# An attention and feed-forward layer on one core: the last unit of the output projection stands four steps later, between two products of the feed-forward tail

## The reference, cut to what matters

```python
q, k, v = x @ Wq[h], x @ Wk[h], x @ Wv[h]                  # (b, h, 1024, 64)
attn = softmax(causal(q @ k.T / sqrt(64)))
heads = attn @ v                                           # 16 heads side by side: (b, 1024, 1024)
y  = x + heads @ Wo
y  = layernorm(y, eps=1e-3) * gamma + beta
x1 = layernorm(x + y, eps=1e-5)
gate, up = x1 @ w_gate.T / 127, x1 @ w_up.T / 127
ffn = (silu(gate) * up) @ w_down.T / 127
out = layernorm(x1 + ffn, eps=1e-5)
```

## Time and profile before

| | |
|---|---|
| median of three runs | 1456.25 us |
| the profiled execution: time, and span from first to last instruction | 1458.17 us, 1456.4 us |
| PE busy | 1409.0 us, 97% of the span |
| DVE, ACT, POOL busy | 71%, 69%, 68% |
| mean granted TensorE clock | 0.991 |
| start of block 9, of block 10 | 769.7, 856.9 us |

### The profile page before, as it was taken

One profiled execution on the slowest core, in us unless ns is written; L12 is line 12 of the kernel. 1 busy time (PEld: TensorE's weight loads), 2 busy tenths in 40 slices (PEclk: granted clock), 3 DMA queues, 4 the chain that ended last, 5 costly groups with the idle time before them and its releaser, 6 DMA issues.

```text
span 1456.4 us, 23825 instructions
## 1 busy us (share of the span) xinstructions
PE 1409.0 (97%) x7976; PEld 1231.7 (85%) x7976; DVE 1031.7 (71%) x2747; ACT 1002.1 (69%) x1924; POOL 984.9 (68%) x926
## 2 busy tenths in 40 slices
PE   7899999999999999999999999999999999999876
PEld 6788888888888888888888888888888888888766
DVE  7777776767676766777667676776767677677864
ACT  4777777877676676867668676676767668676534
POOL 4665666556676775867768586775867768588744
PEclk9999999999999999999999999999999999999998
DMA  3323222323342132322243122132313223121000
GB/s 130 102 81 93 62 67 95 117 52 90 103 123 73 52 95 59 110 54 58 74 117 95 52 61 72 56 120 59 95 44 110 74 60 95 51 64 55 23 12 30
DMA packets 61241, 110.46 MB, mean 76 GB/s; under 512 B 16256, under 2 KB 41600, under 8 KB 61120
## 3 DMA queue, kind: packets, MB, share of 16 engines
q1 hardware_dynamic: 61120, 108.94, 25.2%
HBM read 60.95 MB, written 13.89 MB: 51 GB/s over the span
## 4 chain that ended last, share of the span: by engine, by line
PE 73%; ACT 11%; DVE 8%; POOL 4%; issue 3%; DMA 1%; SPq 0%; ACTq 0%; POOLq 0%
PE bank L798 22%; PE bank L771 15%; PE bank L671 8%; PE bank L747 8%; PE bank L734 7%; PE bank L696 5%; PE bank L833 5%; PE bank L845 3%; ACT probs_hi L987 2%; POOL probs_lo L1428 2%; ACT probs L984 2%; ACT y_tail L1023 1%; ACT Q L967 1%; POOL h_lo L1470 1%; ACT K L967 1%
## 5 line engine op out<-in xcount | busy, mean ns | idle before, releaser
L1428 POOL TENSOR_TENSOR probs_lo<-probs,probs_hi 128x512 fp32r<-128x512 f32 x576 | 747.6, 1305 | 415.1 <-ACT probs_hi L987 412.5
L984 ACT ACTIVATE probs<-bank 128x512 f32<-128x512 f32 x576 | 344.2, 598 | 299.6 <-DVE bank L1185 217.8
L771 PE MATMUL bank<-Q,K 128*128 128x512 f32 (+3 forms) x1536 | 385.9, 353 | 3.4 <-ACT probs_hi L987 2.6
L987 ACT ACTIVATE probs_hi<-bank 128x512 fp32r<-128x512 f32 x576 | 342.2, 594 | 0.0
L771 PEld LDWEIGHTS bank<-Q,K 128*128 128x128 f32 x1536 | 252.1, 190 | 33.6 <-ACT probs_hi L987 6.2
L747 PE MATMUL bank<-K,Q 128*128 128x512 f32 (+3 forms) x768 | 245.5, 362 | 3.9 <-DMA Q<-Q 3.3
L1169 DVE CUSTOM_DVE_ANT_0 bank<-bank,mask_keys_free 128x128 f32<-128x128 f32 (+3 forms) x512 | 243.2, 506 | 4.7 <-PE bank L747 4.2
L798 PE MATMUL bank<-probs_hi,VH 128*128 128x512 f32 (+3 forms) x768 | 232.6, 343 | 7.9 <-POOL probs_lo L1428 7.2
L798 PE MATMUL bank<-probs_lo,VH 128*128 128x512 f32 (+3 forms) x768 | 234.7, 346 | 0.0
L798 PE MATMUL bank<-probs_hi,VL 128*128 128x512 f32 (+3 forms) x768 | 234.7, 346 | 0.0
L1185 DVE TENSOR_TENSOR bank<-bank,mask_queries_free 128x256 f32<-128x256 f32 (+1 forms) x320 | 119.4, 373 | 129.4 <-PE bank L771 128.9
(11 more groups left out here) (173 smaller groups left out, 2230.9 us busy)
## 6 DMA issues: line engine op xcount, KB each, us to landing
Q<-Q SPq DMA_DIRECT2D x64, 256.0 KB, 3.7
K<-K SPq DMA_DIRECT2D x64, 256.0 KB, 3.6
recip_bc<-recip_scratch SPq DMA_DIRECT2D x62, 256.0 KB, 3.4
wh<-w_scratch SPq DMA_DIRECT2D x12, 768.0 KB, 4.3
wl<-w_scratch SPq DMA_DIRECT2D x12, 768.0 KB, 5.8
wo_quad<-wo SPq DMA_DIRECT2D x16, 256.0 KB, 2.9
y<-x SPq DMA_DIRECT2D x16, 256.0 KB, 3.8
x_tail<-x SPq DMA_DIRECT2D x13, 256.0 KB, 4.4
```

The source lines that it names most:

```text
L771: last = mm(bk[:, at:at + cols], KX[:, n, P * i:P * i + P], QX[:, n, q0:q0 + cols], start=(KX is K1 and at == 0), stop=(KX is K2 and at + ...
L984: A(pe_[:, g % 2, :], stb[g % 2][:, :], ACT.Exp).then_inc(exp_done, 1)
L987: A(ph[:, g % RING, :], stb[g % 2][:, :], ACT.Exp).then_inc(hi_done, 1)
L1428: G.tensor_tensor(pl[:, g % RING, :], pe_[:, g % 2, :], ph[:, g % RING, :].bitcast(F32), ALU.subtract).then_inc(lo_done, 1)
```

## The change

The last unit of the output projection (u3) moves from step 21 to step 25 in blocks 1 to 14. In the blocks with a tail it then stands between the second `t_up` (23) and the second `t_down` (26). Its waits follow: in blocks 5 to 14 it waits for `h1`, the last reader of `misc[1]`; the second `t_up` no longer waits for `y_added` of u3 (but in the last block), the third does. `y_add` of u3 moves with it, from DVE's step 22 to step 26, and `load_wo` from SP's step 23 to 27 (but in the last block), as it waits for the unit.

```diff
-WO_AT, WO_AT_LAST = [12, 14, 15, 21], [11, 13, 15, 16]
+WO_AT, WO_AT_LAST = [12, 14, 15, 25], [11, 13, 15, 16]
@@ the step of SP
                 if s == 23 and live:
                     recip_store(QH * it + 1)
-                    load_wo(it)
                 if s == 24 and live:
                     recip_load(QH * it + 1)
                 if s == (EARLY_T[1] + 1 if it == NIT - 1 else 25) and live:
                     max_to_row(QH * it + 3)
+                if s == (23 if it == NIT - 1 else 27) and live:
+                    load_wo(it)
@@ wo_unit, u == 3
                 elif it == NIT - 1:
                     pe.wait_ge(y_added, 4 * wi + 2)
+                elif running(it):
+                    pe.wait_ge(tdve[0], ND * (it - TAIL_LAG) + DV["h1"])
                 else:
                     pe.wait_ge(proj_lo, 2 * proj_unit(it + 1, 0, 2) + 2)
@@ t_up, r > 0
                     pe.wait_ge(tdve[g], ND * n + DV[f"y2{r - 1}"])
                     if g == 0 and r == 1:
-                        pe.wait_ge(y_added, 4 * it)
                         if it + 1 < NIT:
                             pe.wait_ge(proj_lo, 2 * proj_unit(it + 1, 0, 3) + 2)
+                        else:
+                            pe.wait_ge(y_added, 4 * it)
+                    elif g == 0 and it + 1 < NIT:
+                        pe.wait_ge(y_added, 4 * it)
```

## The result

| | before | changed |
|---|---|---|
| median of five runs | 1456.58 us (1454.54 to 1459.19) | 1464.11 us (1461.38 to 1466.79) |
| ratio | | 1.0047, 95% interval 1.0037 to 1.0058 |
| profiled execution, its span | 1458.17, 1456.4 us | 1461.38, 1459.6 us |
| mean granted clock | 0.991 | 0.992 |

The change makes the kernel 0.47% slower by the ratio, which is 6.8 us; the medians are 7.5 us apart. The forecast was 1462.3 us (+6.0), between 1456 and 1467, and slower with a chance of 0.75.

What follows compares the result with a forecast made beforehand. PE's queue (97% busy) was taken as the bound, so only its waits count. Blocks 5 to 14 gave +4.4 us and blocks 1 to 4 +1.6, so 1456.25 + 6.0 = 1462.3 us, range 1456 to 1467.

Steps and rivals of the forecast that it cites:

- Wait A: Step 23, blocks 1 to 14: PE newly waits for POOL's low part of step 21 before products with V, 0.25 us.
- Wait B: Step 25, blocks 5 to 14: the moved unit newly waits for h1 from DVE, 0.57 us a block.
- Wait C: Step 26, blocks 5 to 14: PE's existing wait for h_lo at the second t_down goes, 0.38 us a block.
- Blocks 1 to 4: No tail here: +0.63 us each in blocks 1 and 3, +0.19 each in 2 and 4, together +1.6.
- The 0.15 at the products of step 25: Blocks 1 to 4: added wait because steps 22 to 24 lack filler and step 23's softmax starts from a late DVE.
- The late mask: DVE's addition to y delays step 26's mask; step 28 adds 0.23 us in blocks 1 and 3, 0.51 in 2 and 4.
- the wait ahead of head 3: Blocks 2 and 4: PE's wait for SP's row of maxima, 0.72 us, fully covered by the unit in step 25.
- the 87.6 to 87.7 that were to be the sign: Time in us from the start of block 9 to block 10 expected after the change, instead of 87.2.
- The rival of late row sums in blocks 4, 8 and 12: Late stores on SP's queue delay row sums, holding DVE in step 31: adds 4.5 us, 1466.8; chance 0.12.
- ACT's copy of step 26: copy_out now waits for the unit but ends before the mask that the exponential needs, so it costs nothing.
- The faster rival: Waits on POOL and h1 do not come, old waits at t_down and for maxima go: 5.2 us less, 1451.0; chance 0.09.
- The rival of no change: The h1 wait replaces the t_down wait; POOL wait and late mask cost nothing: about +0.5 us, 1456.8; chance 0.14.

Runs made afterwards that it cites:

- step22: The kernel before with the last unit in step 22 in place of 21; block 9 took 87.23 us, as before (one run).
- two_units: Changed kernel, blocks 1 to 4 as before; in 5 to 14 u3 writes misc[0], third unit moves from step 15 to 21; 1452.32 us, ratio 0.9962 to before.
- expfirst: Changed kernel with ACT's exponentials of step 21 ahead of the emptying of the fourth projection unit, blocks 1 to 14; 1467.87 us, ratio 1.0071 to before.
- bank0: Changed kernel with the moved unit in misc[0] in place of misc[1], waiting for the chain's first DVE instruction; 1457.08 us, ratio 1.000 to before.
- load27: The kernel before with only SP's load of Wo moved from step 23 to 27; block 9 took 87.25 us, before 87.23 (one run).
- step26: Changed kernel with the unit in step 26, its addition in step 27, load of Wo in step 28; block 9 took 87.73 us (one run).

## Why the prediction was right

**The ground.** That nothing would change but PE's waits held: unit and matmuls took the same time in the new place (1.54 us, and 0.20 behind it that left against 0.18 that came back), and all steps but 21 to 28 stayed within about 0.03 us.

**Wait A** (forecast 0.25, measured +0.38 in step 23 of all 14 blocks). The mechanism was right: POOL's low part of step 21 ends, and PE starts right behind it. step22 and two_units show that one filler in step 21 or 22 removes it, and expfirst shows that ACT's order holds it up. The size was a third short. PE stood 827.29 - 827.00 = 0.29 us (826.71 and 0.29 for two matmuls, which is what the same two take before, 827.57 to 827.86), and the first matmul after the wait then took 0.33 us to the next start where the others take 0.23.

**Wait B** (0.57, measured 0.68). PE stood 833.49 - 832.91 = 0.58 (832.67 and two matmuls, 0.24, give 832.91), and 0.10 more went in the unit's own matmuls, 1.99 us in place of the 1.89. bank0 shows it by itself: -0.66 a block.

**Wait C** (0.38 removed, measured 0.49). The down product stood 0.38 us; with it went 0.11 of its slow restart (835.33 to 835.55 before, 0.22 us to the next start; 836.88 to 837.00 now). So the same term of about 0.1 us was left out of all three. In a sum of two new waits and one removed it does not cancel: a steady block was forecast at +0.44 and measured at +0.54, ten of them at +4.4 and +5.46.

**Blocks 1 to 4** (forecast +1.6, measured +1.10). Block by block the changed kernel took +0.47, -0.06, +0.49 and +0.20, where I had +0.63, +0.19, +0.63 and +0.19. A came in with 0.39 in place of 0.25. The 0.15 at the products of step 25 did not come (+0.01). The late mask cost less than forecast in blocks 1 and 3: step 28 grew by 0.08 to 0.10 and not by 0.23. In block 1 its products start 4.02 us after the scores of step 26 (163.57 to 167.59) where I had 4.11, and PE reaches them after 3.78 (167.12 + 0.23 = 167.35) where I had 3.60: that sum left out the 0.18 that the scores behind the unit take longer. In block 2 the wait ahead of head 3 went, -0.72 net of the 0.18 behind the unit. It is absent in every kernel here with the unit in step 25 of these blocks, but in step22 too, which has no unit there, so what the unit is worth at this place is not shown. Since that wait differs between executions, by 0.5 us in block 4 between before and load27, the part of blocks 2 and 4 can't be given more sharply than some tenths.

**The total.** Blocks 5 to 14 came out 1.1 us above the forecast and blocks 1 to 4 0.5 us below, so some of the closeness of +6.0 to the measured +6.56 is luck. The steady block of 87.77 lies just above the 87.6 to 87.7 that were to be the sign.

**SP, the copy and the clock.** load27 shows SP's part at nothing. The rival of late row sums in blocks 4, 8 and 12 did not come: block 8 grew by 0.52 like its neighbours. Its first store goes out at 748.46 us and its first reload at 750.63 (forecast 748.1 and 750.3), and its row sums at 753.82, 0.91 later than before, of which 0.89 is how much later PE's scores of step 30 start, too. The next quarter of Wo is needed some 50 us after its load and not 60, which changes nothing. The granted clock is 1.00 from 58 to 1390 us, as before, with the two new waits in it. The forecast leaned on ACT's copy of step 26 being covered; in block 9 it ends at 836.17, 0.38 us ahead of the mask (836.13 + 0.42 = 836.55) that the exponential needs. With the unit one step later it is not covered, as step26 shows.

**The faster rival** failed where it was said to: `h1` comes 833.44 - 829.99 = 3.45 us after the scores of step 24, to the hundredth what before had, so losing 0.69 us of DVE's work in step 22 did not speed it. With a wait that needs only the first instruction of that chain the rival's gain in step 26 is there to be had (bank0), but 0.38 of its 0.49 us pays for A until step 21 is filled again (two_units).

**The rival of no change** had as its sign that steps 21 to 23 shrink by the full 1.72 us. They shrank by 1.36, where my sum had 1.47.

## What to carry to other kernels

In a kernel whose engines run one order written by hand, count a filler's value at both ends: what it covers where it stands and what it will cover where it goes, each as ready time against reach time, read from starts. A filler moved into a gap brings a wait of its own with it; here the unit was to cover a chain and had to wait for the end of that same chain, because of the bank it wrote. Take the resource that is free earliest in the gap, and leave something in the place that was emptied.

## What the runs showed of the hardware that I had not expected

A wait of PE costs about 0.1 us more than the time in which it stands, since the first matmuls after it come more slowly: 0.33 us in place of 0.23 after wait A, 1.99 in place of 1.89 for the unit after wait B, 0.22 in place of 0.12 after wait C. Each of the three was seen in all ten steady blocks. What makes it was not tested. One thing in the traces fits a guess at the load of the weights: behind wait B the unit's first weight load starts at 833.49, together with its first matmul, and in bank0, where the unit does not wait, the load starts at 829.64, 0.12 ahead of the matmul at 829.76. Behind waits A (827.29) and C (835.33, before) the two start together as well.
